# A windowed-attention block on one core: the deviation's spread on 64-column tiles and the qkv projections on 128 stationary columns

## The reference

```python
xn = _ln2d(x, norm1_g, norm1_b)                 # over the 64 channels
xn = jnp.roll(xn, (-4, -4), (2, 3))
windows = _window_partition(xn, 8)              # 64 windows of 64 tokens
attn_out = _mha(windows, in_w, in_b, out_w, out_b)   # qkv, softmax over 64 keys, 8 heads
attn_out = attn_out @ proj_w.T + proj_b
y = x + jnp.roll(_window_reverse(attn_out, 8, 16, 16, 16), (4, 4), (2, 3))
z = _ln2d(y, norm2_g, norm2_b)
z = gelu(einsum('bchw,oc->bohw', z, fc1_w) + fc1_b)
z = einsum('bchw,oc->bohw', z, fc2_w) + fc2_b
return y + z
```

## Time and profile before

| | |
|---|---|
| median of 3 runs | 87.61 us (86.75 to 88.52) |
| the profiled execution | 87.22 us, of which the span of its instructions is 85.2 us |
| TensorE busy | 79.6 us, 1786 matmul records |
| weight loads | 48.0 us, 1786 |
| VectorE, ScalarE, GpSimd busy | 64.7, 53.0, 46.8 us |
| chain that ended last | TensorE 65%, VectorE 18%, issue 8%, DMA 3%, ScalarE 2% |

### The profile page before, as it was taken

The page is one execution under the profiler, slowest core; times in us unless marked ns, Lnnn a source line. Parts: engine busy times, 40 slices in busy tenths (PEclk is TensorE's granted clock), DMA queues, the critical chain, the costliest instruction groups (busy, mean ns, idle before and its releaser), DMA issues.

```text
span 85.2 us, 4265 instructions
## 1 busy us (share of the span) xinstructions
PE 79.6 (93%) x1786; PEld 48.0 (56%) x1786; DVE 64.7 (76%) x208; ACT 53.0 (62%) x89; POOL 46.8 (55%) x58
## 2 busy tenths in 40 slices
PE   5999999889999999799999999999999999999950
PEld 5987757555865767467566637465464423533420
DVE  4999998969789989989789999997943944333260
ACT  0396798879888476588288356664587664725400
POOL 7988829989862972997634675787204041300000
PEclk9999999999999999999999999999999999999998
DMA  0799600121101122101021120000000000032042
GB/s 19 203 331 439 258 31 8 36 66 33 53 32 53 51 84 78 53 1 38 32 100 56 52 64 6 8 0 8 0 8 0 0 0 0 13 118 86 38 162 84
DMA packets 3490, 5.75 MB, mean 67 GB/s; under 512 B 944, under 2 KB 1712, under 8 KB 3344
## 3 DMA queue, kind: packets, MB, share of 16 engines
q1 hardware_dynamic: 2608, 3.08, 10.9%
q10 hardware_dynamic: 864, 2.40, 7.3%
HBM read 2.66 MB, written 1.05 MB: 44 GB/s over the span
## 4 chain that ended last, share of the span: by engine, by line
PE 65%; DVE 18%; issue 8%; DMA 3%; ACT 2%; SPq 1%; DVEq 0%; ACTq 0%
PE ps_s L333 14%; PE ps_u L426 6%; PE ps_u L499 5%; DVE row_max L656 4%; PE ps_m L307 4%; PE ps_s L483 4%; PE ps_t L333 3%; PE ps_t L483 3%; DMA masked<-qk 3%; PE ps_o L467 3%; PE ps_m L483 2%; PE ps_t L409 2%; PE ps_m L297 2%; PE ps_o L499 2%; PE ps_o L442 2%
## 5 line engine op out<-in xcount | busy, mean ns | idle before, releaser
L1058 POOL TENSOR_TENSOR max_x<-max_t,early 128x512 bf16<-128x512 bf16 x14 | 14.7, 1048 | 10.6 <-DVE max_t L669 10.6
L656 DVE TENSOR_REDUCE row_max<-ps_s 128x16 f32<-128x1024 f32 x15 | 18.1, 1209 | 2.5 <-PE ps_s L333 2.2
L915 ACT ACTIVATE probs<-ps_t 128x1024 f32<-128x1024 f32 x13 | 13.3, 1023 | 8.8 <-PE ps_t L409 8.4
L333 PE MATMUL ps_s<-masked,qk 32*64 32x256 f32 x240 | 16.9, 387 | 1.0 <-ACT probs L915 0.4
L333 PE MATMUL ps_t<-masked,qk 32*64 32x256 f32 x224 | 15.5, 387 | 0.0
L1067 POOL TENSOR_TENSOR rstd<-y_var,minus_half 128x4 f32<-128x4 f32 x8 | 8.1, 1010 | 9.9 <-DVE y_var L719 9.8
L333 PEld LDWEIGHTS ps_s<-masked,qk 32*64 32x64 f32 x240 | 8.1, 131 | 5.9 <-issue 2.9
L426 PE MATMUL ps_u<-probs,vz 128*32 128x64 f32 x512 | 10.5, 222 | 0.0
L426 PEld LDWEIGHTS ps_u<-probs,vz 128*32 128x32 f32 x512 | 7.9, 109 | 3.1 <-issue 2.7
L1043 POOL TENSOR_TENSOR rstd<-var,minus_half 128x4 f32<-128x4 f32 x8 | 8.3, 1043 | 1.0 <-DVE var L644 0.4
L282 PE MATMUL ps_t<-zeros 128*128 128x128 f32 x32 | 6.9, 376 | 1.0 <-DVE zeros L817 1.0
(11 more groups left out here) (111 smaller groups left out, 150.6 us busy)
## 6 DMA issues: line engine op xcount, KB each, us to landing
masked<-qk SPq DMA_DIRECT2D x38, 32.0 KB, 2.0
x_ch<-x_ch_d ACTq DMA_DIRECT2D x1, 1024.0 KB, 8.0
out_d<-result SPq DMA_DIRECT2D x3, 256.0 KB, 2.5
x_tok<-x_tok_d ACTq DMA_DIRECT2D x1, 512.0 KB, 6.0
masked<-qk SPq DMA_DIRECT2D x8, 64.0 KB, 2.4
late<-late_d ACTq DMA_DIRECT2D x1, 352.0 KB, 5.2
x_tok<-x_tok_d SPq DMA_DIRECT2D x2, 128.0 KB, 3.4
x_tok<-x_tok_d ACTq DMA_DIRECT2D x1, 256.0 KB, 4.8
```

The costliest lines, as they stand in the source:

```text
L333: return nc.tensor.matmul(ps[o:o + L, g, n * TOK:(n + 1) * TOK], qk[r:r + RG, b, w, t], masked[r:r + RG, b, :, w, t], start=(n == 0), stop ...
L656: nc.vector.tensor_reduce(row_max[:, w, 0:16], score_bank(k, w)[:].rearrange("q g (h j) -> q (g h) j", j=L), axis=AX.X, op=ALU.max).then_i ...
L915: nc.scalar.activation(probs[:, w, :], scores_t_bank(k, w)[:].rearrange("q g c -> q (g c)"), ACT.Exp).then_inc(probs_done, 1)
L1058: nc.gpsimd.tensor_tensor(max_x[:, k % 2, w, :].rearrange("q (n i) -> q n i", n=16), bf16_high(max_t[:, w, :]).unsqueeze(1).to_broadcast([ ...
```

## The change

The query and key projection of one image goes through one product with 128 stationary columns (queries on output partitions 0 to 63, keys on 64 to 127) in place of two with 64, on array tiles of 64 rows and 128 columns. The value projection takes 128 tokens of an image as stationary columns in place of twice 64. The spread of the deviation uses two column tiles of 64 for every tile, where tiles 0 to 5 had four of 32. The transposes of x stay on 64x64 tiles. No step changes its place on any engine, and no wait is added or taken away.

```diff
@@ project_qk
                 for w in range(2):
                     r = slice(C * w, C * w + C)
-                    for s in range(2):
-                        ins = nc.tensor.matmul(ps_m[C * s:C * s + C, w, 0:TOK], w_qkv[r, C * s:C * s + C],
-                                               xn[r, k % 2, :], start=True, stop=True, tile_position=(C * w, C * s))
+                    ins = nc.tensor.matmul(ps_m[:, w, 0:TOK], w_qkv[r, 0:2 * C], xn[r, k % 2, :],
+                                           start=True, stop=True, tile_position=(C * w, 0))
                 ins.then_inc(qk_projected, 1)
@@ project_v
                 for n in range(BLK):
                     for w in range(2):
                         r = slice(C * w, C * w + C)
-                        for u in range(2):
-                            t = slice((2 * n + u) * L, (2 * n + u + 1) * L)
-                            ins = nc.tensor.matmul(ps_m[C * u:C * u + C, w, TOK + n * C:TOK + (n + 1) * C],
-                                                   xn[r, k % 2, t], w_qkv[r, 2 * C:3 * C],
-                                                   start=True, stop=True, tile_position=(C * w, C * u))
+                        ins = nc.tensor.matmul(ps_m[:, w, TOK + n * C:TOK + (n + 1) * C],
+                                               xn[r, k % 2, n * P:(n + 1) * P], w_qkv[r, 2 * C:3 * C],
+                                               start=True, stop=True, tile_position=(C * w, 0))
                 ins.then_inc(v_projected, 1)
@@ y_spread
-                cols = 32 if k < TILES - 2 else C
+                cols = C
                 for b in range(BLK):
                     for c in range(0, P, cols):
```

## The result

The changed kernel takes 89.53 us in the median of five runs, the kernel before, on the same chip, 88.1 in its five. The ratio is not that of these two medians (1.016), since they include runs more than 1.5% above the fastest of their kernel, such as one of 115.58 after the change at a granted clock of 0.65, and these are left out of all ratios here. It is 1.0268, 95% interval 1.0201 to 1.0336: slower, by a little more than the 2% that can be told from no change. The profiled execution of the kernel after took 90.01, with a span of 88.0 against 85.2. Three more lines move up by three: L656 is L653, L662 L659, L675 L672.

The account below looks back on a forecast made before the run. TensorE was taken as the bound (busy 93% of the span, 65% of the chain). Terms 0.67 + 0.10 + 0.65 + 0.38 + 0.20 + 0.54 + 0.12 = 2.66 us on 87.4 gave a forecast of 90.0, range 88.4 to 91.3.

Parts of the forecast that it names:

- sum of 2.66: Time added on the path over all slots and the tail, in us; 3.54 without any cover.
- Unit prices: TensorE's cost per reshaped group: projection 0.21 for shape plus 0.17 for paced loads, 0.38; spread 0.27 us.
- Early projections: Projections of tiles 0 to 4: new shape and paced loads, partly hidden in waits, add 0.67 us together.
- tile 0: First tile's projections: +0.05 and +0.17, less 0.11 as the L507 group no longer changes shape: +0.11 us.
- Slot 2: 28.9 to 34.9: projection 5 costs 0.38, mostly hidden by TensorE's 0.45 wait for an exponential; 0.10 us left.
- Slots 3 and 4: Slot 3: projection 0.38 plus spread 0.27, 0.65 us uncovered; slot 4: projection 7, 0.38 us; VectorE waits for L426 in both.
- Spreads of tiles 1 and 2: In the stretch where VectorE runs nearly without a wait: 0.54 us, 0.34 covered by TensorE's idle time, 0.20 paid.
- Spreads of tiles 3 and 4: After 55, where everything is TensorE: both spreads paid in full, 0.54 us.
- Tile 5: Its spread, after 55, already comes from 64x128: 0.16 less a short wait, 0.12 us.
- VectorE as the pace (1): From 28.9 to 55 TensorE's extra time disappears in its waits; 1.33 us left, 88.7; chance 0.18.
- A gain from fewer instructions: Value projections and spreads: each matmul costs engine time, so half as many give 2.6 us back, 84.8; chance 0.06.
- Row-half loads that follow each other (3): Value projection: loads of the two row halves don't overlap, 0.35 more each, some 1.7 us, 91.7; chance 0.06.

Follow-up runs that it names:

- the doubled columns: Kernel after with the value projection's moving columns taken twice, 128 in place of 64, the copy going to unread PSUM; 89.38 us in its single run.
- the second execution: The kernel after, unchanged, profiled once more: 89.11 us, span 87.1.
- the spread ahead: Kernel after with two lines exchanged, so that the spread comes ahead of the slot's last weighing; median 89.15 us, ratio 1.0194 to the kernel before.
- the second execution of before: The kernel before, unchanged, profiled once more: 87.53 us, span 85.4.
- the kernel with the grouped tail: Kernel before with fc1(1, 1) moved directly behind fc1(1, 0), to enter 64x128 once less in the tail; ratio 1.0115 to the kernel before.

## Why the prediction was right

The time was right (90.0 against a median of 89.53 and a profiled execution of 90.01), for the causes that it named. That its sum of 2.66 lies within 0.2 us of the profiled difference of 2.8 is in part luck: the change itself accounts for some 2.4 of it, and the executions added 0.95 (0.21 at the start, 0.33 behind the held maximum, 0.41 by the late DMA) and took off 0.52 by the stall before.

- *Unit prices.* Right. A projection was put at 0.38 (0.21 for the shape, 0.17 for paced loads) and measures 0.361 in slots 2 to 4: 0.204 and 0.157. The 0.157 is 0.05 in each of the last three rounds of L316, as the prediction had it (0.056, 0.112, 0.112 and 0.206 up to L423, where L319 had 0.056, 0.059, 0.058 and 0.158). That loads pace the second and the third is borne out by the doubled columns. The spread was put at 0.27 and measures 0.287; that a change of the columns alone is charged is shown by the spread on the kernel before.
- *Early projections, 0.67.* Too large by some 0.15. The profiled execution has 1.03, of which 0.21 stands ahead of the first projection and 0.33 is the scores' longer wait behind the held maximum; 0.49 is left, and the second execution has 0.53. More than half of the error is tile 0, put at 0.11, which measures 0.02: the small group behind its query projection saves not only the change of shape but its own first load too (0.257 in place of 0.361).
- *Slot 2, 0.10.* 0.51 in the profiled execution, by the late masking DMA; 0.10 in the second, and 0.10 with the projections alone. The slack in front of the exponential hides the projection, as said. That the DMA itself had only little slack, the prediction didn't say.
- *Slots 3 and 4, 0.65 and 0.38.* 0.65 and 0.36; VectorE's transposes wait that much longer.
- *Spreads of tiles 1 and 2, 0.20 paid of 0.54.* 0.20 of 0.57. Each slot runs 0.12 longer, with TensorE busy from end to end and VectorE nearly so.
- *Spreads of tiles 3 and 4, 0.54.* 0.57.
- *Tile 5, 0.12.* Nothing: the spread and the wait behind it take 0.65 together, before as after, so the short wait in front of L448 took all of it. A small term, and mis-sized.
- *Not in the sum:* the stall of 0.52 in the profiled execution of before, which one of after needn't have. It lay in the 87.22 on which the sum was built, and was read there as score time.

**The rivals.** VectorE as the pace (1) falls: its part of the chain went from 18% to 1%, it waits longer in slots 2 to 4, and the stretch that was 28.9 to 55 grew by 1.2 us in the profiled execution, with the DMA's 0.41 and the stall's 0.52 nearly offsetting each other. A gain from fewer instructions (2) falls: 144 records less gave back nothing. The floor of some 25 ns from start to start that the Trainium skill states ("TensorE: Matmul & The Clock Gate", section "Wait — 56ns, not 53.3ns?") would, by an estimate, have made 0.40 us of the 16 records of the old L319; the trace does not agree, they take 0.22 besides leaving. Row-half loads that follow each other (3) would give rounds of 0.23; they are 0.112.

**Not settled.** What the charge for leaving a shape consists of can't be seen in a record. The executions scatter by about 1 us through waits and stalls that aren't the change's, so the 0.36 and 0.29 are known better than the 2.3 us of the ratio.

## What to carry to other kernels

On an engine that is busy without a gap, count the changes of tile shape in its order and the first load behind each, not the instructions: in this kernel fewer, wider matmuls with the same rounds gained nothing, and lost where the wide load took longer than the columns that move under it, and where the group's neighbours had shared its old shape. Price such a change by the distance between starts of neighbouring groups in the trace of before: these prices held to 0.02 us. If one group is to be reshaped, price the group beside it as well: here the second cost nothing once the first had paid.

## What the runs showed of the hardware that had not been expected

**One change of shape costs the same for one group or two.** One projection on 128 columns (either of the two) or both: 0.361 in slots 3 and 4 of three kernels, though the parts differ.

**TensorE stalls without a semaphore, at fixed instruction counts.** The gap shows as "issue", 0.15 to 1.0 us, and not in every execution. The windows from the start up to the stall (length, then busy time and records of PE, PEld, DVE, ACT, POOL) give its count, here for the kernel before, then the one with only the value projection changed, then the one with both projections alone:

```profile
0.00:41.50 41.50, 39.36 (x971) 28.03 (x973) 36.59 (x136) 29.87 (x57) 31.36 (x43) 1.00 0.28 96
```

```profile
0.00:33.40 33.40, 31.91 (x596) 22.57 (x596) 27.58 (x109) 23.16 (x43) 25.28 (x35) 1.00 0.31 107
```

```profile
0.00:49.90 49.90, 47.93 (x1097) 34.64 (x1097) 43.18 (x153) 34.25 (x65) 35.07 (x47) 1.00 0.26 89
```

The run with the query and key projection alone stalls at 596 too, that with the spread ahead at 1097. Counting all instructions of TensorE (loads, matmuls, waits) the stalls stand at 1218, 1473 (the one of 1.0 us), 1985 and 2241, 255, 512 and 256 apart; the second execution of before and the kernel with the grouped tail have further ones at 2497, 2753 and 3010. The traces also hold transfers of instructions, 16 KB each, here in the kernel before (packets, MB, share of 16 engines):

```profile
q8 instruction: 14, 0.23, 1.1%
```

One falls on every 256 of these instructions: the fourth on 1218, the fifth on 1473, and so on. In all eleven traces TensorE passes the eight counts from 1218 to 3010 no sooner than 1.25 us after the end of the fitting packet; every stall ends 1.25 to 1.67 after it, and where the packet ended longer ago there is none. So the traces bear out that TensorE waits there for instructions; no run that moves these packets was made.

**VectorE held by GpSimd.** In the kernel after VectorE's maximum L659 took 0.59, and ended as GpSimd's multiply did; first VectorE's timeline, then GpSimd's:

```profile
20.39 0.59 DVE L659 TENSOR_TENSOR row_max<-row_max 128x16 f32<-128x16 f32 x1
```

```profile
20.34 0.61 POOL L1047 TENSOR_TENSOR xhat<-x_tok,rstd 128x256 f32<-128x256 f32 x1
```

In the kernel before the same operation took 0.17, and over all traces it takes 0.13 to 0.18 but for the two that started behind such a multiply:

```profile
19.98 0.17 DVE L662 TENSOR_TENSOR row_max<-row_max 128x16 f32<-128x16 f32 x1
```

The second is in the kernel with the projections alone: 0.40, to 0.03 us after GpSimd's end. Where it started ahead of the multiply it was not held (0.17 at 16.44 in the kernel after, with the multiply from 16.53). Beside GpSimd's power function on small tiles it kept its 0.17.

**The masking DMA** lands 1.7 to 3.5 us after its issue in the kernel after (median 1.9). Where TensorE's scores wait for it, as above for the queries of tiles 3 and 4 (3.37, and 1.97 in the second execution), that made 0.4 us of the time.
